# Three of four weight sums moved from VectorE to accumulating transfers that GpSimd issues, in a cross-attention and mixture-of-experts kernel

## What is computed

```python
router_input = jnp.concatenate([h, modality_ratio], axis=-1)
gate_scores = softmax(router_input @ gate_w + gate_b)
top_val, top_idx = jax.lax.top_k(gate_scores, TOP_K)          # TOP_K = 2
pre = einsum('bsd,edf->ebsf', h, w1) + b1                      # act: tanh / gelu / silu
out = einsum('ebsf,efd->ebsd', act, w2) + b2
for i in range(TOP_K):
    moe_out = moe_out + top_val[..., i:i + 1] * expert_out[top_idx[:, 0, i], batch_idx]
x = x + moe_out                                                # h = layernorm(x)
```

## Time and profile before

| | |
|---|---|
| median of 3 runs | 404.01 us (403.53 to 404.82) |
| the profiled execution | 403.35 us, of which 401.5 us are the span that the profile covers |
| TensorE matmul busy | 384.8 us (96%) |
| VectorE busy | 347.2 us (86%) |
| ScalarE busy | 195.2 us (49%) |
| GpSimd busy | 53.6 us (13%) |
| granted TensorE clock over the span | 0.996 |

### The profile page before, as it was taken

How to read it: one execution, slowest core, us unless ns; L and a number is a source line. 1 busy time by engine, 2 the same in 40 slices (tenths; PEclk the granted TensorE clock), 3 DMA queues, 4 the chain that set the end, 5 groups by cost and what they waited for, 6 DMA issues and landing times.

```text
span 401.5 us, 5230 instructions
## 1 busy us (share of the span) xinstructions
PE 384.8 (96%) x1860; PEld 303.4 (76%) x1860; DVE 347.2 (86%) x539; ACT 195.2 (49%) x253; POOL 53.6 (13%) x70
## 2 busy tenths in 40 slices
PE   1999999999999999999989999999999999999996
PEld 1435737888888888888867888888888888888885
DVE  8799869999999799999999997694997865949973
ACT  3568645174447625651846263343476333424720
POOL 8648400530000000063100000000000000000000
PEclk9999999999999999999998999999999999999999
DMA  8996049441006585000000499400055880000112
GB/s 316 411 408 282 2 137 376 169 148 61 2 0 205 177 299 211 2 0 2 0 0 2 147 379 385 189 0 2 0 176 192 241 283 2 0 0 2 53 52 106
DMA packets 23981, 54.39 MB, mean 135 GB/s; under 512 B 1776, under 2 KB 1808, under 8 KB 23824
## 3 DMA queue, kind: packets, MB, share of 16 engines
q1 hardware_dynamic: 23888, 54.01, 37.5%
q10 hardware_dynamic: 64, 0.02, 0.0%
HBM read 49.83 MB, written 4.19 MB: 135 GB/s over the span
## 4 chain that ended last, share of the span: by engine, by line
PE 84%; DVE 9%; ACT 2%; issue 2%; DMA 1%; ACTq 1%; POOL 0%; DVEq 0%; POOLq 0%
PE ps L1638 43%; PE ps L1607 34%; PE ps L1401 4%; DVE xres L867 2%; DVE hT_lo L876 1%; DMA b1n<-in_L_ffn_b_dram 1%; DVE bn L796 1%; DVE xres L1089 1%; PE ps L1433 1%; DVE w_lo L992 1%; PE ps L1389 1%; DVE raw L1023 1%; PE ps L1333 0%; DVE q L830 0%; DVE act_f L1058 0%
## 5 line engine op out<-in xcount | busy, mean ns | idle before, releaser
L643 ACT ACTIVATE w_hi<-raw 128x1024 fp32r<-128x1024 f32 x88 | 88.5, 1053 | 45.6 <-DVE raw L1023 22.6
L992 DVE TENSOR_TENSOR w_lo<-raw,w_hi 128x1024 fp32r<-128x1024 f32 x88 | 103.6, 1219 | 0.6
L1638 PE MATMUL ps<-hT_hi,w_hi 128*128 128x512 f32 x256 | 99.9, 390 | 0.0
L1638 PE MATMUL ps<-hT_hi,w_lo 128*128 128x512 f32 x256 | 99.6, 389 | 0.0
L1638 PE MATMUL ps<-hT_lo,w_hi 128*128 128x512 f32 x256 | 99.6, 389 | 0.0
L1607 PE MATMUL ps<-w_hi,a_hi 128*128 128x512 f32 x224 | 88.2, 394 | 2.6 <-DVE w_lo L992 2.5
L1607 PE MATMUL ps<-w_lo,a_hi 128*128 128x512 f32 x224 | 87.7, 391 | 0.0
L1607 PE MATMUL ps<-w_hi,a_lo 128*128 128x512 f32 x224 | 87.6, 391 | 0.0
L731 ACT ACTIVATE act_f<-ps,b1T 128x512 f32<-128x512 f32 x32 | 22.1, 690 | 109.1 <-PE ps L1638 109.0
L1638 PEld LDWEIGHTS ps<-hT_hi,w_hi 128*128 128x128 f32 x256 | 48.1, 188 | 10.2 <-issue 0.2
L1638 PEld LDWEIGHTS ps<-hT_hi,w_lo 128*128 128x128 f32 x256 | 48.1, 188 | 10.0
(11 more groups left out here) (156 smaller groups left out, 369.7 us busy)
## 6 DMA issues: line engine op xcount, KB each, us to landing
raw<-in_L_ffn_w_dram SPq DMA_DIRECT2D x64, 512.0 KB, 5.6
raw<-in_ctx_dram SPq DMA_DIRECT2D x16, 512.0 KB, 11.5
xres<-in_x_dram SPq DMA_DIRECT2D x8, 512.0 KB, 9.5
out_dram<-xres SPq DMA_DIRECT2D x16, 256.0 KB, 4.2
b2row<-in_L_ffn_b_dram SPq DMA_DIRECT2D x4, 512.0 KB, 6.8
gate_rows<-in_L_ffn_gate_w_dram SPq DMA_DIRECT2D x1, 1536.0 KB, 18.3
small<-in_L_xattn_x_scale_dram ACTq DMA_DIRECT2D x2, 0.0 KB
small<-in_L_xattn_x_zp_dram ACTq DMA_DIRECT2D x2, 0.0 KB
```

The costliest lines, as they stand in the source:

```text
L643: nc.scalar.activation(w_hi[n % SLOTS][:, 2 * c:2 * c + 2, :], region(q)[:, 2 * c:2 * c + 2, :], ACT.Copy).then_inc(w_hi_ready, 1)
L992: V.tensor_tensor(w_lo[n % SLOTS][:, 2 * c:2 * c + 2, :], region(n % QUARTERS)[:, 2 * c:2 * c + 2, :], w_hi[n % SLOTS][:, 2 * c:2 * c + 2, ...
L1638: last = T.matmul(ps[:, G1_BANK + f % 2, :], w[q % SLOTS][:, k % TT, fs], h[:, k, :], start=n == 0, stop=n == 3 * KT - 1)
```

## The change

On **GpSimd** the sums t3, t2 and t4 of every pair become transfers with an accumulating write: `add_regions(into, other, done)` issues two of 128x1024 elements (512 KB) from SBUF to SBUF that add one region to another. Each sum has a semaphore of its own (`t3_in`, `t2_in`, `t4_in`). GpSimd waits for the operands ahead of each, and its order is written out: all sums of the first pair, t3 of the second, tile 0, t2 and t4 of the second, tiles 1 to 3, the sums of the other pairs.

On **VectorE** the three instructions are gone; t1 stays. As the transfers can only add, blocks get other signs: s1 becomes a subtraction, s2 and s4 become `scalar_tensor_tensor` with a factor of -1, and the results of the right half are taken with `minus_gate`, a negated copy of the gates (one small instruction more for each sequence). The order of the second pair's second product changes: t1 comes ahead of the low part of tile 2, `result(1, 1)` moves behind `w_lo` of quarter 7, and the low part of tile 3 and the router's steps move behind `w_lo` of quarter 8.

On **ScalarE** the waits of `w_hi_chunk` name the new semaphores.

```diff
@@ gpsimd
-            for t in range(TT):
+            def add_regions(into, other, done):
+                for c in range(2):
+                    G.dma_start(region(into)[:, 2 * c:2 * c + 2, :], region(other)[:, 2 * c:2 * c + 2, :],
+                                accum_op=ALU.add).then_inc(done, 16)
+            def t3_sum(p):
+                for slot in (2, 3, 4, 5):
+                    pool.wait_ge(raw_in[slot], 16 * (2 + 2 * p + 2))
+                add_regions(8, 9, t3_in)
+            def t2_sum(p):
+                pool.wait_ge(t3_in, 32 * p + 32)
+                pool.wait_ge(w_lo_ready, 2 * (QUARTERS * p + 4) + 2)
+                add_regions(6, 8, t2_in)
+            def t4_sum(p):
+                pool.wait_ge(t2_in, 32 * p + 32)
+                pool.wait_ge(w_lo_ready, 2 * (QUARTERS * p + 5) + 2)
+                add_regions(10, 6, t4_in)
+            t3_sum(0)
+            t2_sum(0)
+            t4_sum(0)
+            t3_sum(1)
+            second_h_tile(0)
+            t2_sum(1)
+            t4_sum(1)
+            for t in range(1, TT):
                 second_h_tile(t)
+            for p in range(TOP_K, PAIRS):
+                t3_sum(p)
+                t2_sum(p)
+                t4_sum(p)
@@ vector
             def t1_sum(p):
-                dve.wait_ge(t_ready, 4 * p + 3)
+                dve.wait_ge(t4_in, 32 * p + 32)
                 dve.wait_ge(w_lo_ready, 2 * (QUARTERS * p + 6) + 2)
-                V.tensor_tensor(region(7), region(9), region(6), ALU.subtract).then_inc(t_ready, 1)
+                V.tensor_tensor(region(7), region(6), region(9), ALU.subtract).then_inc(t1_ready, 1)
@@ result
-                    V.scalar_tensor_tensor(out=xt, in0=ps[:, bank + j, :], scalar=gate[:, p * TT + t:p * TT + t + 1],
+                    signed = (gate, minus_gate)[half]
+                    V.scalar_tensor_tensor(out=xt, in0=ps[:, bank + j, :], scalar=signed[:, p * TT + t:p * TT + t + 1],
@@ order of the first product
-                    elif f == 1:
-                        if p > 0:
-                            t3_sum(p)
...
-                        if p > 0:
-                            t2_sum(p)
                     elif f == 4:
                         w_lo_quarter(q + 5)
-                        if p > 0:
-                            t4_sum(p)
-                        else:
-                            t3_sum(p)
-                    elif f == 5 and p == 0:
-                        t2_sum(p)
-                    elif f == 6 and p == 0:
-                        t4_sum(p)
@@ order of the second product
                 result(p, 0)
+                t1_sum(p)
                 if p == 1:
                     h_lo(1, 2)
-                t1_sum(p)
-                result(p, 1)
+                else:
+                    result(p, 1)
+                w_lo_quarter(q + 7)
                 if p == 1:
+                    result(p, 1)
+                late_lo(p, 1)
+                w_lo_quarter(q + 8)
+                if p == 1:
+                    h_lo(1, 3)
                     router_bias(1)
                     dot_scores()
                     score_steps()
-                w_lo_quarter(q + 7)
-                late_lo(p, 1)
-                if p == 1:
-                    h_lo(1, 3)
-                w_lo_quarter(q + 8)
                 result(p, 2)
```

More of the change, by code:

```diff
@@ L199, in build @@
         gate = sb("gate", [P, PAIRS * TT], F32)
+        minus_gate = sb("minus_gate", [P, PAIRS * TT], F32)
         gate_rows = sb("gate_rows", [P, D * NE], F32)
@@ L269, in build @@
         late_lo_ready = sem("late_lo_ready")
-        t_ready = sem("t_ready")
+        t1_ready = sem("t1_ready")
+        t2_in = sem("t2_in")
+        t3_in = sem("t3_in")
+        t4_in = sem("t4_in")
         g2_done = sem("g2_done")
@@ L637, in w_hi_chunk @@
                     act.wait_ge(g2_done, 2 * NP * p + 2 * (q - 7))
-                t_sum = {8: 1, 6: 2, 10: 3, 7: 4}.get(q)
-                if t_sum:
-                    act.wait_ge(t_ready, 4 * p + t_sum)
+                if q == 6:
+                    act.wait_ge(t2_in, 32 * p + 32)
+                elif q == 7:
+                    act.wait_ge(t1_ready, p + 1)
+                elif q == 8:
+                    act.wait_ge(t3_in, 32 * p + 32)
+                elif q == 10:
+                    act.wait_ge(t4_in, 32 * p + 32)
                 else:
@@ L987, in gate_values @@
                 then(V.tensor_tensor(gate[:, 8 * b + 4:8 * b + 8], mid, a, ALU.mult))
+                then(V.tensor_scalar(minus_gate[:, 8 * b:8 * b + 8], gate[:, 8 * b:8 * b + 8], -1.0, None, ALU.mult))
             def w_lo_chunk(n, c):
@@ L1038, in s1_sum @@
                 dve.wait_ge(s3_ready, TT * p + k + 1)
-                V.tensor_tensor(act_f[:, k, 2 * P:4 * P], act_f[:, k, 2 * P:4 * P], act_f[:, TT + k, 2 * P:4 * P],
-                                ALU.add).then_inc(s1_ready, 1)
+                V.tensor_tensor(act_f[:, k, 2 * P:4 * P], act_f[:, TT + k, 2 * P:4 * P], act_f[:, k, 2 * P:4 * P],
+                                ALU.subtract).then_inc(s1_ready, 1)
             def s1_lo(p, k):
@@ L1050, in s2_sum @@
                 dve.wait_ge(s1_lo_ready, TT * p + k + 1)
-                V.tensor_tensor(act_f[:, k, 2 * P:4 * P], act_f[:, TT + k, 2 * P:4 * P], act_f[:, k, 0:2 * P],
-                                ALU.subtract).then_inc(s2_ready, 1)
+                V.scalar_tensor_tensor(out=act_f[:, k, 2 * P:4 * P], in0=act_f[:, TT + k, 2 * P:4 * P], scalar=-1.0,
+                                       in1=act_f[:, k, 0:2 * P], op0=ALU.mult, op1=ALU.subtract
+                                       ).then_inc(s2_ready, 1)
             def s4_sum(p, k):
@@ L1057, in s4_sum @@
                 dve.wait_ge(a_lo_ready, KT * p + TT + k + 1)
-                V.tensor_tensor(act_f[:, TT + k, 0:2 * P], act_f[:, TT + k, 0:2 * P], act_f[:, k, 2 * P:4 * P],
-                                ALU.subtract).then_inc(s4_ready, 1)
+                V.scalar_tensor_tensor(out=act_f[:, TT + k, 0:2 * P], in0=act_f[:, TT + k, 0:2 * P], scalar=-1.0,
+                                       in1=act_f[:, k, 2 * P:4 * P], op0=ALU.mult, op1=ALU.subtract
+                                       ).then_inc(s4_ready, 1)
             def late_lo(p, j):
@@ L1231, in _ @@
                             pass
-                    elif f == 1:
-                        if p > 0:
-                            t3_sum(p)
-                        else:
-                            pass
                     elif f == 2 and p == 0:
```

## The result

The changed kernel takes **409.25 us** (median of 3 runs, 408.97 to 410.85), against 404.01: a ratio of 1.0138 with a 95% interval of 1.009 to 1.0186. A later comparison gave 409.27 against 404.39, ratio 1.0115 (1.0093 to 1.0138). The change costs about 5 us. The profiled execution took 410.85 us, of them 409.1 in the span.

A forecast was written before the change was run, and what follows sets the result against it. TensorE, 96% busy, was taken to bound the kernel, with about 4.1 us to gain in the second pair. Order 1.5, clock 0.8 and tile 1 2.0 gave +4.3 on 404.0: 408.3 us, range 403.4 to 415.0.

The forecast's parts named there:

- Removed work worth 0: All pairs: taking twelve VectorE sums away, 27 us busy, gains 0; in the second pair VectorE had caught up at 193.59.
- The 4.1 us named as all there is to gain: Second pair, ahead of block product 3: a 2.52 us wait for `w_lo` of quarter 7 plus 1.6 us of clock loss.
- The order: Second pair's second product: old stall replaced by waits ahead of turning tile 3 and block product 4, +1.5 us.
- Tile 1: Second pair: GpSimd's tile 1 queues behind t2's landing and t4's issue, so TensorE turns it late, +2.0 us.
- The clock: Second pair: clock falls during one of the two new stalls, costing between 0 and 1.6 us, taken as +0.8.
- Pair 0: First pair: three sums of 8.2 us in a row end at 115.1, ahead of t1 at 116.32; worth 0.
- Relief: Rival, second pair: the stall goes and nothing replaces it, 399.9 us; needs result 1 out by 207.9; chance 0.11.
- The slow transfers: Rival: at 10.7 us a sum, tile 1 and pair 0's t1 are late, 417.4 us; decides from about 9.3; chance 0.13.
- the prediction's sign of being wrong: Prediction wrong if a sum takes under 6 us or over 9.3, or the second pair is under 90 us.
- The quick transfers: Rival, second pair: tile 1 is in time, order and clock alone cost, 405.5 to 407.1 us; chance 0.14.
- The estimate by the formula: GpSimd's transfers: 2.0 us plus bytes over 436 GB/s; by it the tile 1 term is 0 and the sum 406.3.
- Tile 0 did not starve: Rival, second pair: without t2's gap on VectorE, tile 0 ends near 179.9, delaying t2 and tile 1, 413.0 us; chance 0.08.

The follow-up runs named there:

- sums_only: The changed kernel with VectorE's old order of the second product put back: 405.82 us against 404.46, ratio 1.0033.
- the two good orders: t1 and result 1 first, router's steps behind result 3: on the kernel before 402.23 us, on the changed one with tile 1 ahead of t4 402.39.
- order_only: The kernel before with only the new order of the second pair's second product, all sums on VectorE: 407.79 us against 404.46, ratio 1.008.
- result1_first: The changed kernel with the second pair's result 1 right behind t1, ahead of tile 2's low part: 407.55 us, ratio to before 1.0062.
- router_late: The changed kernel with tile 3's low part and the router's steps of the second pair behind result 2: 407.15 us, ratio to before 1.0072.
- a copied sum: The changed kernel with the accumulation taken out, so the twelve sums are copies and outputs differ: 408.58 us against 404.91, one execution.
- after_again: The changed kernel once more, unaltered: 409.27 us against 404.39 for the kernel before.
- tile1_first: The changed kernel with tile 1 ahead of t4 of the second pair on GpSimd: 408.79 us, ratio to before 1.0099.

## Why the prediction was right

408.3 us was forecast, +4.3; measured are 409.25, +5.2, and +4.9 in the later comparison. The mechanism held: work worth nothing removed, a new order that costs, a late tile 1, a clock loss behind the longer wait. Two of its sizes were off in opposite directions, so that the sum came so close is in part luck. Point by point, in the second pair of the profile, +5.62:

- **Removed work worth 0: right.** sums_only met the old wait at its old 2.52 us, the two good orders, with and without the transfers, differ by 0.02 us, and the other pairs stayed at 81.6 to 81.8. The reason given, that VectorE had caught up at 193.59, is in the profile after as the same 0.20 us of waiting. The 4.1 us named as all there is to gain count 1.6 for the clock, of which sums_only shows only about 0.7 as lengthening the pair while result 2 stays where it is.
- **The order, forecast +1.5: measured +1.66** in order_only, with a wait of 2.05 us ahead of turning tile 3 (2.1 forecast). The wait ahead of block product 4 was 3.50 in the change (3.5 forecast), and 1.90 in order_only, where the slow block product 3 took up the other 1.6. The causes are those named. result1_first and router_late took out one wait each and confirmed them one by one.
- **Tile 1, forecast +2.0: 1.3 measured.** Three parts were off and partly cancel. Tile 0 ended 0.7 us sooner in the pair than in the earlier trace rows. A sum took 7.4 us and not 8.2: the base was taken too long (a copied sum takes 4.55, not 5.6), and the addition's share was about right (2.9 for 2.6). GpSimd's issue of t4 with the tile took 3.0 and not 2.25: the tile starts 1.13 us behind the first issue, where twice SyncE's 0.37 had been taken, and takes 1.85 and not 1.5.
- **The clock, forecast +0.8 between 0 and 1.6: mis-sized.** Behind block product 4's start the pair was longer by 2.66 in the profiled execution, by 1.75 in after_again, and by 0.1 in order_only, with the clock at 1.00. That it may be hidden or not was right; the upper end was too low, as it came from the one dip of the kernel before, 1.6 us. This term is more than the whole difference between forecast and profile, and tile 1 takes part of it back (clock +1.9, order +0.2, tile 1 -0.7: together the 1.3 us between 5.62 and 4.3, within rounding).
- **Pair 0: right at 0.** Three sums one behind the other began at 92.01, t4 went out at 108.43 and block product 3 did not wait; the first pair takes 81.83.
- **The rivals.** Relief, the faster case, was said to need result 1 out in time. It was not, but the condition was too weak: result1_first had it out in time and was still 3.1 us above before, since result 2 stayed late behind the router's steps. The slow transfers needed 9.3 us a sum. None of the sums that something waits for reached that: the longest, t3 of the first pair, has 8.8 us from its issue to t2's. t3 of the second to the fourth pair did pass it, beside the weight loads, and by its letter the prediction's sign of being wrong (a sum of over 9.3 us) came up there, without a cost. The quick transfers would have been the copies. The estimate by the formula of the Trainium skill, page DMA: Bandwidth & Descriptors, section Anatomy of one DMA, 4.4 us for 1 MB, agrees with the copied sum (4.55) and not with the accumulated one (7.43); by it tile 1 would have been in time, and it was not.
- **Tile 0 did not starve:** it took 4.58 us, as in the earlier trace rows. It did not need a gap left by VectorE's sum. VectorE's timeline, in the changed kernel and, in the last two rows, in the kernel before:

```profile
173.28 2.37 DVE L1037 TENSOR_TENSOR w_lo<-raw,w_hi 128x1024 fp32r<-128x1024 f32 x2
175.55 1.28 DVE L1054 TENSOR_TENSOR a_lo<-act_f,a_hi 128x256 fp32r<-128x256 f32 x1
...
174.47 2.95 DVE L1011 TENSOR_TENSOR raw<-raw 128x2048 f32<-128x2048 f32 x1
181.99 2.95 DVE L1017 TENSOR_TENSOR raw<-raw 128x2048 f32<-128x2048 f32 x1
```

Tile 0 ended at 176.56; before, tile 0 ended at 175.28 and tile 1 at 182.80. Each time the instruction of VectorE under way just then was longer than its kind: 1.28 us in place of 0.42, and twice 2.95 in place of 2.28. So a tile seems to get in between two instructions of VectorE, at the cost of the second, whatever that one is; no run tests this. That VectorE holds GpSimd up, which the Trainium skill states on the page SBUF — State Buffer, section Who interferes with whom, agrees with the 4.58 us; which instruction it gets in ahead of is not settled.

What stays open is when the clock falls. In the profiles it stayed at 1.00 behind waits of 1.90, 2.33 and 2.52 us and fell behind others of 1.92 and 2.52; behind the six of 2.04 to 2.06, all ahead of turning tile 3, it fell three times (order_only, after_again, tile1_first); at or behind the four of 2.77 to 3.51 it always fell. No experiment here controls it.

## What to carry to other kernels

Before work is moved off a busy engine, find the last place before the stall where that engine itself waited: work ahead of that place is free already, and taking it away moves nothing. When an instruction is pulled forward in a hand-written order, list everything that waits for what it overtakes; here one small result held up a turned tile, ScalarE and the next result. And try the order alone: it cost two thirds of the loss, and in a better form it gave the only gain, 2 us, without any transfer.

## What the hardware showed that I had not expected

- The same wait does not have the same price. Behind 2.52 us the clock fell to 1.2 GHz in the kernel before and stayed at 1.00 in sums_only; behind 3.50 us it was low for over five microseconds in the change, some 2.6 us lost. Behind 1.92 us in after_again it fell and some 1.7 us were lost; behind 1.90 in order_only it stayed at 1.00. A wait can cost from its own length to nearly twice that.
- An accumulating transfer from SBUF to SBUF writes at about half the rate of a copy, 197 to 211 GB/s against 389, and two issues of it keep GpSimd for 1.74 us and not 1.05. A sum of two regions of 1 MB takes 7.4 us, three times VectorE's 2.3, and more beside the weight loads. In these kernels it gained nothing even where nothing waited for it.
